# Beta held eight times per partition, so that the four transfers that add it move 4 KB rows

## The chip, the cores and the metric

The kernel runs on one core of a Trainium2 chip. The metric is the device time of one execution in microseconds (us), and a kernel's time is the median of its runs.

## What is computed

The input x has the shape (4, 1024, 128), in f32. Two layers follow one another. Each is added to its own input. Cut to what matters, in f32 throughout:

```python
# layer 1: attention without a softmax, 16 heads of 8
h = layernorm(x)
q, k, v = elu(h @ Wq + bq) + 1, elu(h @ Wk + bk) + 1, h @ Wv + bv
k = k / sqrt(sum(k * k, over a head) + 1e-6)
attn = q @ (k^T @ v)                    # per batch and head
y = h + attn @ Wo + bo
x = x + (y - mean(y)) / sqrt(var(y) + 1e-6) * gamma + beta

# layer 2: the 768 rows of each batch with the highest score go through a small product
h = layernorm(x)
scores = h @ w_router
top = top_k(scores, 768)
x = x + h.at[top].set(gelu(h[top] @ w_block))
```

The change touches the last line of layer 1 alone: how the sum x + beta comes to be.

## The kernel before

**Tiles.** A tile is 128 rows of one batch, one row per partition, 128 f32 values (512 B) in each. A batch has 8 tiles (`T`), and half a batch, 4 tiles (`TH`), is a unit `u`; there are 8 units (`U`). All work runs unit by unit. Every engine has its own list of steps, written out by hand at the end of its block, and semaphores tie them together, so no scheduler chooses an order.

**The steps on TensorE (PE).** Units are transposed (`transpose_h`), multiplied with the key and query weights (`k_proj`, `q_proj`), and once both halves of a batch have their normalised keys `attention_matrix(b)` (L1228) forms the product of keys and rows. `values`, `attention_out` and `y_half` (L1252, L1253) then give y.

**What the change touches.** The buffer `xb_sb` holds a second copy of x, loaded from DRAM in four transfers of one batch each (512 KB, L317, semaphores `xb_in[b]`) at the end of the list of loads of the SP queue. Four transfers issued from GpSimd (POOL) then add beta to it, one per batch (`add_beta(b)`, L394, semaphores `xb_set[b]`). Such a transfer reads `beta_sb` and `xb_sb`, adds, and writes `xb_sb`. `beta_sb` holds beta once in each partition (128 x 128, 64 KB in all, loaded at L312), and the source of the add names it eight times with a step of zero, so that a partition's row is made of eight runs of 512 B.

**What waits for them.** POOL waits for `beta_in` and `xb_in[0]` ahead of `add_beta(0)`, and its next steps are queued behind that wait: `scale_k(0)` and `scale_k(1)` (L400), which normalise the keys that `attention_matrix(0)` needs. The order on POOL is `add_beta(0)`, `scale_k(0)`, `scale_k(1)`, `add_beta(1)`, `add_beta(2)`, `scale_k(2)`, `scale_k(3)`, `add_beta(3)`, `scale_k(4)`, `roots2(0)` (L413), and so on. `scale_k(u)` itself waits for `key_norms(u // 2)` of VectorE (DVE, L799 and L801). The sums x + beta are read by POOL's `residual(0)` (L420, batch 0) and by DVE's `residual(u)` (L886), which wait for `xb_set[u // 2]`.

Of the kernel before, what the change touches and what calls it, by code (L numbers as in the profile page):

```python
# [12 lines left out]
P = 128  # L13
# [7 lines left out]
def preln_linear_attention_mod_ffn(nc, x, wq, bq, wk, bk, wv, bv, wo, bo, gamma, beta, w_router, w_block, out):  # L21
# [9 lines left out]
    B, L, D = x.shape  # L31
    assert D == P and HEADS * DEPTH == D and L % (2 * TH * P) == 0
    T = L // P
# [18 lines left out]
    with ExitStack() as ctx:  # L52
        def sb(name, shape, dt=F32):
            return ctx.enter_context(nc.sbuf_tensor(name, shape, dt))

        def sem(name):
            return ctx.enter_context(nc.semaphore(name))
# [3 lines left out]
        xb_sb = sb("xb_sb", [P, B * T, D])  # L61
# [46 lines left out]
        wz_sb = sb("wz_sb", [P, P + 1])  # L108
        wz_c = sb("wz_c", [P, P + 1])
        gamma_sb = sb("gamma_sb", [P, P])  # L110
        beta_sb = sb("beta_sb", [P, P])

        bias_rows = sb("bias_rows", [P, 3 * P])

# [14 lines left out]
        bias_in, bo_in, gamma_in, beta_in = sem("bias_in"), sem("bo_in"), sem("gamma_in"), sem("beta_in")  # L129
# [170 lines left out]
        @block.sync  # L300
        def _(sp):
            for u in range(U):
                b, a = u // 2, TH * (u % 2)
                if u == 0:
                    for h in range(2):
                        t = TH // 2 * h
                        sp.dma_start(x_sb[:, t:t + TH // 2, :], x_v[b, :, t:t + TH // 2, :]).then_inc(x0_in[h], 16)
                    sp.dma_start(w_sb[:, 2 * P:3 * P], wv).then_inc(w_in, 16)
                else:
                    sp.dma_start(x_sb[:, TH * u:TH * u + TH, :], x_v[b, :, a:a + TH, :]).then_inc(x_in[u], 16)  # L310
            sp.dma_start(wo_sb[:], wo).then_inc(wo_in, 16)
            sp.dma_start(beta_sb[:], beta.partition_broadcast(P)).then_inc(beta_in, 16)  # L312
            sp.dma_start(gamma_sb[:], gamma.partition_broadcast(P)).then_inc(gamma_in, 16)
            sp.dma_start(wz_sb[:, 0:P], w_block).then_inc(wz_in, 16)
            sp.dma_start(wz_sb[:, P:P + 1], w_router.unsqueeze(1)).then_inc(wz_in, 16)
            for b in range(B):
                sp.dma_start(xb_sb[:, T * b:T * b + T, :], x_v[b]).then_inc(xb_in[b], 16)  # L317
            for n, u in enumerate(MERGE_ORDER):
                sp.wait_ge(merged, n + 1)
                b, a = u // 2, TH * (u % 2)  # L320
                n = TH if u != LAST else TH // 2
                sp.dma_start(out_v[b, :, a:a + n, :], x_sb[:, TH * u:TH * u + n, :]).then_inc(out_stored, 16)
            sp.wait_ge(out_stored, 16 * (U + 1))

        @block.gpsimd
        def _(pool):
# [45 lines left out]
            def first_roots(h):  # L372
                _, m2 = stats(bn1, 2 * h, 2 * h + 2)
                t0, t1 = 2 * h, 2 * h + 2
                pool.wait_ge(first_stats_done, h + 1)
                link(nc.gpsimd.tensor_scalar(var1[:, t0:t1], m2, 1.0 / D, LN_EPS, ALU.mult, ALU.add))
                nc.gpsimd.tensor_tensor(r1[:, t0:t1], var1[:, t0:t1], minus_half[:].to_broadcast([P, 2]),
                                        ALU.pow).then_inc(first_r_done, 1)

            def roots1(g):  # L380
                us = ROOT_GROUPS[g]
                t0, t1 = TH * us[0], TH * us[-1] + TH
                _, m2 = stats(bn1, t0, t1)
                pool.wait_ge(x_stats, us[-1])
                link(nc.gpsimd.tensor_scalar(var1[:, t0:t1], m2, 1.0 / D, LN_EPS, ALU.mult, ALU.add))
                nc.gpsimd.tensor_tensor(r1[:, t0:t1], var1[:, t0:t1], minus_half[:].to_broadcast([P, t1 - t0]),
                                        ALU.pow).then_inc(r1_done, 1)

            def add_beta(b):

                if b == 0:
                    pool.wait_ge(beta_in, 16)
                pool.wait_ge(xb_in[b], 16)
                nc.gpsimd.dma_start(xb_sb[:, T * b:T * b + T], beta_sb[:].unsqueeze(1).to_broadcast([P, T, D]),  # L394
                                    accum_op=ALU.add).then_inc(xb_set[b], 16)

            def scale_k(u):
# [43 lines left out]
            roots1(4)  # L441
            masks()
            add_beta(0)
            scale_k(0)
            scale_k(1)
            add_beta(1)
            add_beta(2)
            scale_k(2)
            scale_k(3)
# [276 lines left out]
        def _(dve):  # L726
# [108 lines left out]
            def variances3(u):  # L835
                t0, t1 = TH * u, TH * u + TH
                _, m2 = stats(bn3, t0, t1)
                dve.wait_ge(x1_stats_done, u + 1)
                nc.vector.tensor_scalar(var3[:, t0:t1], m2, 1.0 / D, LN_EPS, ALU.mult, ALU.add).then_inc(var3_done, 1)  # L839
# [669 lines left out]
```

## Time and profile before

| | before |
|---|---|
| median of 3 runs | 91.2 us (91.19, 91.20, 91.83) |
| the profiled execution | 91.51 us |
| its span in the trace | 89.8 us |
| outside the span | 1.7 us |
| PE busy | 79.9 us (89%) |
| VectorE (DVE) busy | 80.9 us (90%) |
| ScalarE (ACT) busy | 66.9 us (75%) |
| GpSimd (POOL) busy | 52.8 us (59%) |
| granted TensorE clock, mean | 0.992 |

The profile is taken from one execution. Times in it are microseconds from the start of its span. PE stands for matmuls and PEld for weight loads. "SPq" marks the issuing of a DMA on the SP queue, and a row of a DMA says how long the issuing took. How long the transfer was under way is the time "to landing". The chain of work that ended last is followed back from the last instruction: what is not on it, or waits behind it, costs nothing.

### The profile page before, as it was taken

To read this page: it belongs to the slowest core of one execution; us is meant where nothing else is said; L and a number is where in the kernel's file an instruction comes from. 1 tells how busy PE (TensorE), PEld (TensorE's weight loads), DVE (VectorE), ACT (ScalarE), POOL (GpSimd) and SP (SyncE) were. 2 spreads that over 40 slices of the span, in tenths; PEclk is the share of its full clock that TensorE was granted. 3 is DMA by queue.
4 is the path that set the end of the run, shared out by engine and by line. 5 is a ranking of instruction groups with operands and counts; after the bars stand their busy time and mean duration, and the time that the engine had idled before them with its cause. 6 is when DMAs were issued, how large, how long until landed. Compare 5 with 4: busy or idle time off the path is not lost.

```text
span 89.8 us, 2397 instructions
## 1 busy us (share of the span) xinstructions
PE 79.9 (89%) x816; PEld 68.4 (76%) x816; DVE 80.9 (90%) x258; ACT 66.9 (75%) x186; POOL 52.8 (59%) x79
## 2 busy tenths in 40 slices
PE   4998689999999999999999599999999797999700
PEld 1335656976797997999999599999998797779600
DVE  4368999999797897999999999999999999999960
ACT  5003599998999996753539799999799696998700
POOL 5265885989992997659770979769838400000000
PEclk9999999999999999999999999999999999999996
DMA  0899969970999999900000000000000000348456
GB/s 24 233 256 319 280 168 319 290 189 7 143 127 140 139 143 136 112 10 0 0 0 0 0 7 0 0 4 7 0 4 0 0 7 10 107 121 236 138 149 180
DMA packets 18113, 8.99 MB, mean 100 GB/s; under 512 B 819, under 2 KB 18102, under 8 KB 18102
## 3 DMA queue, kind: packets, MB, share of 16 engines
q1 hardware_dynamic: 13232, 6.49, 26.7%
q0 software_dynamic: 4160, 2.10, 21.5%
q10 hardware_dynamic: 710, 0.26, 1.1%
q8 instruction: 6, 0.10, 0.4%
q14 instruction: 5, 0.04, 0.1%
HBM read 4.66 MB, written 2.10 MB: 75 GB/s over the span
## 4 chain that ended last, share of the span: by engine, by line
PE 46%; DVE 41%; issue 4%; ACT 3%; DVEq 1%; POOL 1%; ACTq 0%
DVE beats L918 11%; PE bank L1219 7%; PE bank L1211 7%; PE bank L1152 6%; DVE xb_sb L886 5%; DVE x_sb L941 5%; DVE bn L893 4%; PE bank L1252 4%; PE bank L1228 4%; PE bank L1253 4%; PE bank L1188 3%; PE bank L1271 3%; DVE beats L927 2%; DVE bn L818 2%; DVE x_sb L853 2%
## 5 line engine op out<-in xcount | busy, mean ns | idle before, releaser
L918 DVE TENSOR_SCALAR beats<-s_row,s_col 128x1024 bf16<-128x1024 f32 (+7 forms) x32 | 15.5, 541 | 0.0
L595 ACT ACTIVATE norm_sb<-xb_sb,shift,gain 128x128 f32<-128x128 f32 x32 | 13.2, 507 | 2.7 <-DVE shift L847 2.7
L1252 PE MATMUL bank<-M_sb,qT 128*128 128x128 f32 x64 | 12.5, 277 | 0.0
L1253 PE MATMUL bank<-back,hT 128*128 128x128 f32 x64 | 12.4, 275 | 0.0
L413 POOL TENSOR_TENSOR r<-var,minus_half 128x4 f32<-128x4 f32 x8 | 8.1, 1025 | 5.8 <-DVE var L833 5.5
L400 POOL TENSOR_TENSOR k_sb<-k_sb,k_rnorm 128x512 f32<-128x512 f32 x8 | 9.3, 1252 | 2.7 <-DVE k_rnorm L801 2.7
L426 POOL TENSOR_TENSOR r<-var,minus_half 128x4 f32<-128x4 f32 x8 | 9.1, 1194 | 2.9 <-DVE var L839 2.9
L1252 PEld LDWEIGHTS bank<-M_sb,qT 128*128 128x128 f32 x64 | 9.7, 192 | 0.2 <-ACT M_sb L558 0.2
L1253 PEld LDWEIGHTS bank<-back,hT 128*128 128x128 f32 x64 | 9.7, 192 | 0.0
L588 ACT ACTIVATE x_sb<-bank,r 128x128 f32<-128x128 f32 x32 | 9.2, 383 | 0.2 <-DVE s_col L901 0.2
L1219 PEld LDWEIGHTS bank<-w_c,hT 128*128 128x128 f32 x56 | 6.9, 192 | 2.1 <-ACT hT L513 1.1
L1271 PE MATMUL bank<-wz_c,hT 128*128 128x129 f32 x64 | 8.5, 278 | 0.0
L1219 PE MATMUL bank<-w_c,hT 128*128 128x128 f32 x56 | 7.3, 277 | 0.9 <-ACT hT L513 0.9
L1211 PE MATMUL bank<-hT,w_c 128*128 128x512 f32 x16 | 8.0, 593 | 0.0
L1228 PE MATMUL bank<-k_sb,norm_sb 128*128 128x128 f32 x64 | 7.8, 275 | 0.0
L1271 PEld LDWEIGHTS bank<-wz_c,hT 128*128 128x128 f32 x64 | 7.7, 192 | 0.0
L886 DVE SCALAR_TENSOR_TENSOR xb_sb<-bank,r,xb_sb 128x128 f32<-128x128 f32 x28 | 7.6, 338 | 0.0
L1228 PEld LDWEIGHTS bank<-k_sb,norm_sb 128*128 128x128 f32 x64 | 7.5, 192 | 0.0
L1292 PE MATMUL bank<-ident,beats 128*128 128x128 bf16 x108 | 6.8, 219 | 0.6 <-DVE dropped L936 0.6
L394 POOL DMA_DIRECT2D xb_sb<-beta_sb x4 | 7.0, 2060 | 0.1
L1152 PE MATMUL bank<-idle 128*128 128x512 bf16 x14 | 5.8, 601 | 1.3 <-DVE idle L735 1.3
L1292 PEld LDWEIGHTS bank<-ident,beats 128*128 128x128 bf16 x108 | 6.2, 98 | 0.9 <-DVE beats L918 0.8
(132 smaller groups left out, 216.7 us busy)
## 6 DMA issues: line engine op xcount, KB each, us to landing
xb_sb<-in_L_attn_x_dram SPq DMA_DIRECT2D x4, 512.0 KB, 6.8
xb_sb<-beta_sb POOLq DMA_DIRECT2D x4, 512.0 KB, 8.4
x_sb<-in_L_attn_x_dram SPq DMA_DIRECT2D x7, 256.0 KB, 5.2
out_dram<-x_sb SPq DMA_DIRECT2D x7, 256.0 KB, 2.3
x_sb<-in_L_attn_x_dram SPq DMA_DIRECT2D x2, 128.0 KB, 2.7
out_dram<-x_sb SPq DMA_DIRECT2D x1, 128.0 KB, 2.4
out_dram<-x_sb ACTq DMA_DIRECT2D x1, 128.0 KB, 2.5
w_sb<-in_L_attn_Wq_dram ACTq DMA_DIRECT2D x1, 64.0 KB, 2.5
```

The source lines that it names most:

```text
L400: nc.gpsimd.tensor_tensor(out_keys, keys, norms, ALU.mult).then_inc(keys_pool, 1)
L595: last = nc.scalar.activation(norm_sb[:, t], xb_sb[:, t], ACT.Identity, bias=shift3[:, t:t + 1], scale=gain3[:, t:t + 1])
L886: last = nc.vector.scalar_tensor_tensor(out=xb_sb[:, n], in0=bank_of(("y", u))[:, t * P:(t + 1) * P], scalar=r2[:, n:n + 1], in1=xb_sb[:, ...
L918: nc.vector.tensor_scalar(beats[:, b % 2, J, P * J:T * P], s_row[:, b, P * J:T * P], s_J, None, ALU.is_le).then_inc(beats_done, 1)
L1152: nc.tensor.matmul(bank[:, 7, :], idle16[:, 0:P], idle16[:], start=True, stop=True)
L1211: nc.tensor.matmul(take(("q", u)), w_c[:, 0:P], hT[:, u], start=True, stop=True).then_inc(q_full, 1)
L1219: last = nc.tensor.matmul(o[:, t * P:(t + 1) * P], hT[:, u, t * P:(t + 1) * P], w_c[:, P:2 * P], start=True, stop=True)
L1228: last = nc.tensor.matmul(o[:, 0:P], norm_sb[:, T * b + t], k_sb[:, 2 * b + t // TH, t % TH], start=(t == 0), stop=(t == T - 1))
L1252: nc.tensor.matmul(o, qT[:, u, t * P:(t + 1) * P], M_sb[:, b], start=True, stop=False)
L1253: last = nc.tensor.matmul(o, hT[:, u, t * P:(t + 1) * P], back[:], start=False, stop=True)
L1271: last = nc.tensor.matmul(o[:, j * (P + 1):(j + 1) * (P + 1)], hT[:, u, t * P:(t + 1) * P], wz_c[:], start=True, stop=True)
L1292: last = nc.tensor.matmul(o[:, n * P:(n + 1) * P], beats[:, b % 2, J, I * P:(I + 1) * P], ident16[:], start=(I == J), stop=(I == T - 1))
```

## The change

`beta_sb` grows from 128 x 128 to 128 x 8 x 128: beta lies eight times, one after the other, in each partition (4 KB per partition, 512 KB in all). Its load reads the same 512 B of DRAM eight times for each partition, and it is issued later: behind gamma and the two loads of `wz_sb`, right ahead of the four loads of `xb_sb`. In `add_beta` both sides are now named as flat rows of 1024 values, so that source and destination of a partition are one run of 4 KB each. Sum, semaphores, and the order of all other work stay.

```diff
-        beta_sb = sb("beta_sb", [P, P])
+        beta_sb = sb("beta_sb", [P, T, D])
...
             sp.dma_start(wo_sb[:], wo).then_inc(wo_in, 16)
-            sp.dma_start(beta_sb[:], beta.partition_broadcast(P)).then_inc(beta_in, 16)
             sp.dma_start(gamma_sb[:], gamma.partition_broadcast(P)).then_inc(gamma_in, 16)
             sp.dma_start(wz_sb[:, 0:P], w_block).then_inc(wz_in, 16)
             sp.dma_start(wz_sb[:, P:P + 1], w_router.unsqueeze(1)).then_inc(wz_in, 16)
+            sp.dma_start(beta_sb[:], beta.partition_broadcast(P).unsqueeze(1).to_broadcast([P, T, D])).then_inc(beta_in, 16)
             for b in range(B):
                 sp.dma_start(xb_sb[:, T * b:T * b + T, :], x_v[b]).then_inc(xb_in[b], 16)
...
-                nc.gpsimd.dma_start(xb_sb[:, T * b:T * b + T], beta_sb[:].unsqueeze(1).to_broadcast([P, T, D]),
+                nc.gpsimd.dma_start(xb_sb[:, T * b:T * b + T].rearrange("p t d -> p (t d)"), beta_sb[:].rearrange("p t d -> p (t d)"),
                                     accum_op=ALU.add).then_inc(xb_set[b], 16)
```

The SP queue, which issues the loads, from the load of `wo_sb` to the stores (a row: line, what, shape of the destination; "-" before, "+" after):

```order
 L311 DMA wo_sb<-in_L_attn_Wo_dram 128x128
-L312 DMA beta_sb<-in_L_attn_beta_dram 128x128
-L313 DMA gamma_sb<-in_L_attn_gamma_dram 128x128
-L314 DMA wz_sb<-in_L_ffn_w_block_dram 128x128
-L315 DMA wz_sb<-in_L_ffn_w_router_dram 128x1
+L312 DMA gamma_sb<-in_L_attn_gamma_dram 128x128
+L313 DMA wz_sb<-in_L_ffn_w_block_dram 128x128
+L314 DMA wz_sb<-in_L_ffn_w_router_dram 128x1
+L315 DMA beta_sb<-in_L_attn_beta_dram 128x8x128
 L317 DMA xb_sb<-in_L_attn_x_dram 128x8x128 x4
```

Beta's load went from the place behind `wo_sb` to the place ahead of `xb_sb`, and became eight times as large. The three loads that it was ahead of each stand one place earlier.

POOL, from the last of the masks to the second `scale_k` pair:

```order
 L368 AFFINE_SELECT head_mask<-head_mask 128x128
-L394 DMA xb_sb<-beta_sb 128x8x128
+L394 DMA xb_sb<-beta_sb 128x1024
 L400 TENSOR_TENSOR k_sb<-k_sb,k_rnorm 128x512 x2
-L394 DMA xb_sb<-beta_sb 128x8x128 x2
+L394 DMA xb_sb<-beta_sb 128x1024 x2
 L400 TENSOR_TENSOR k_sb<-k_sb,k_rnorm 128x512 x2
```

Nothing moved on POOL. The four adds keep their places and change their shape. PE, DVE and ACT have the same lists as before.

## Rows read from the trace of the kernel before

**Rows 1.** The page: the span, and the chain that ended last by engine.

```profile
span 89.8 us, 2397 instructions
...
PE 46%; DVE 41%; issue 4%; ACT 3%; DVEq 1%; POOL 1%; ACTq 0%
```

**Rows 2.** The chain that ended last, in order of time: start, us, what.

```profile
20.05 0.86 PE bank L1211 x2
...
34.85 0.24 PE bank L1234 x2
...
43.62 0.77 POOL r L413
```

**Rows 3.** Timeline of PE: start, us, engine, line, operation, out<-in.

```profile
23.36 1.04 PE L1188 MATMUL bank<-ident,norm_sb 128*128 128x128 f32 x8
24.23 1.95 PE L1228 MATMUL bank<-k_sb,norm_sb 128*128 128x128 f32 x16
```

**Rows 4.** Timeline of the SP queue's issuing.

```profile
9.62 0.43 SPq L315 DMA_DIRECT2D wz_sb<-in_L_ffn_w_router_dram  x1
10.09 5.39 SPq L317 DMA_DIRECT2D xb_sb<-in_L_attn_x_dram  x4
```

**Rows 5.** Timeline of POOL around the adds, idle time before and its releaser in brackets.

```profile
19.92 1.75 POOL L394 DMA_DIRECT2D xb_sb<-beta_sb  x1
21.11 2.71 POOL L400 TENSOR_TENSOR k_sb<-k_sb,k_rnorm 128x512 f32<-128x512 f32 x2
23.17 3.74 POOL L394 DMA_DIRECT2D xb_sb<-beta_sb  x2
28.53 2.11 POOL L400 TENSOR_TENSOR k_sb<-k_sb,k_rnorm 128x512 f32<-128x512 f32 x2 [1.62 <-DVE k_rnorm L801]
30.59 1.53 POOL L394 DMA_DIRECT2D xb_sb<-beta_sb  x1
31.93 1.31 POOL L400 TENSOR_TENSOR k_sb<-k_sb,k_rnorm 128x512 f32<-128x512 f32 x1
...
37.58 1.27 POOL L420 TENSOR_TENSOR xb_sb<-norm_sb,xb_sb 128x512 f32<-128x512 f32 x1
```

**Rows 6.** Timeline of DVE: the norms that `scale_k` waits for.

```profile
20.72 0.29 DVE L801 SCALAR_TENSOR_TENSOR k_rnorm<-k_tmp,k_seed 128x128 f32<-128x128 f32 x1
...
31.55 0.29 DVE L801 SCALAR_TENSOR_TENSOR k_rnorm<-k_tmp,k_seed 128x128 f32<-128x128 f32 x1
```

**Rows 7.** DMA issues: out<-in, queue, count, KB each, median us to landing.

```profile
beta_sb<-in_L_attn_beta_dram SPq DMA_DIRECT2D x1, 64.0 KB, 3.9
...
wz_sb<-in_L_ffn_w_block_dram SPq DMA_DIRECT2D x1, 64.0 KB, 3.0
```

**Rows 8.** Line L317, the first load of xb_sb alone: issue, and time to landing.

```profile
L317 SPq DMA_DIRECT2D xb_sb<-in_L_attn_x_dram x1: 434/434/434, 10.1 to 10.1; - x1
...
DMA to landing us min/median/max: 5.5/5.5/5.5
```

**Rows 9.** Line L317, the last load of xb_sb alone: issue, and time to landing.

```profile
L317 SPq DMA_DIRECT2D xb_sb<-in_L_attn_x_dram x1: 1619/1619/1619, 13.9 to 13.9; - x1
...
DMA to landing us min/median/max: 6.8/6.8/6.8
```

**Rows 10.** Line L394, the four adds together: time to landing.

```profile
DMA to landing us min/median/max: 6.9/8.4/11.3
```

**Rows 11.** Stretches: bounds, length, busy PE PEld DVE ACT POOL, clock, DMA share, GB/s.

```profile
12.00:12.50 0.50, 0.50 (x7) 0.50 (x6) 0.50 (x3) 0.50 (x2) 0.50 (x1) 1.00 0.52 125
...
15.50:16.00 0.50, 0.50 (x5) 0.50 (x6) 0.50 (x2) 0.50 (x2) 0.50 (x1) 1.00 1.20 291
```

**Rows 12.** DMA queues over the span: packets, MB, their time as share of 16 engines.

```profile
q1 hardware_dynamic: 13232, 6.49, 26.7%
q0 software_dynamic: 4160, 2.10, 21.5%
```

**Rows 13.** DMA queues in the stretch 22 to 39 us: the fetching of instructions.

```profile
q8 instruction: 2, 0.03, 0.7%
q14 instruction: 2, 0.02, 0.2%
```

**Rows 14.** Timeline of DVE: the steps that read x + beta of batches 1 to 3.

```profile
44.06 2.14 DVE L886 SCALAR_TENSOR_TENSOR xb_sb<-bank,r,xb_sb 128x128 f32<-128x128 f32 x8
...
50.63 2.15 DVE L886 SCALAR_TENSOR_TENSOR xb_sb<-bank,r,xb_sb 128x128 f32<-128x128 f32 x8
...
61.30 2.15 DVE L886 SCALAR_TENSOR_TENSOR xb_sb<-bank,r,xb_sb 128x128 f32<-128x128 f32 x8
```

## The prediction

> **What bounds the kernel now.** I read the page first. The span is 89.8 us, and the chain that ended last is PE for 46% and DVE for 41%; POOL holds 1% of it [rows 1]. The chain in order of time then tells what is critical where: from 20.05 to 34.85 us, over all the stretch in which the change acts on POOL's list, every piece is PE, one after the other with nothing between, and POOL's only piece that matters comes at 43.62, a root of 0.77 us [rows 2]. The timeline of PE shows the one step there that needs POOL's work: `attention_matrix(0)` starts at 24.23, and the transposes ahead of it start at 23.36 and are recorded for 1.04, so PE comes to it without a gap [rows 3]. The timeline of POOL shows when its part is done: `add_beta(0)` is issued at 19.92 and takes 1.75, and `scale_k(0)` and `scale_k(1)` run from 21.11 to 23.82 (21.11 + 2.71) [rows 5]. So the keys are there 0.41 us before PE wants them (24.23 - 23.82).
>
> **What the change adds.** Beta's load has 512 KB where it had 64, and all four loads of `xb_sb` are behind it. It takes the slot that the router weights' issue has now, 9.62, or the next one near 10.09 [rows 4]: one load is taken out ahead of it, so it is issued at about 9.6 and the first load of `xb_sb` again near 10.1. The question is how far the landing of `xb_sb` slips.
>
> Now the first load lands at 10.09 + 5.5 = 15.6 [rows 4, 8] and the last at 13.9 + 6.8 = 20.7 [rows 9]. Four loads, three steps between them: 5.1 / 3 = 1.7 us for each 512 KB. Beta's load has the same bytes and the same 512 B pieces, so I take 1.7 for it. From below it is 0: around 12 us the DMA engines are not full, with a share of 0.52 and 125 GB/s against 1.20 and 291 GB/s at 15.5 [rows 11], and a load issued sooner can fill that hole. From above it is 5.5, a whole load from issue to landing, as if nothing overlapped [rows 8]. The first batch of `xb_sb` then lands at 17.3 (15.6 to 21.1), the last at 22.4.
>
> POOL wants batch 0 at 19.92, where it issues `add_beta(0)` today, so at 17.3 there are 2.6 us to spare. Batches 1 and 2 land at about 19.0 and 20.7 and are wanted from 23.17 on; batch 3 lands at 22.4 and is wanted at 30.59 [rows 5]. Cost 0. What hides it is POOL's own list up to 19.92. The cover ends like this: queued behind `add_beta(0)` are the two `scale_k`, and behind those `attention_matrix(0)` on PE. From the issue of the add to `scale_k(0)` are at most 1.19 us today (21.11 - 19.92), the pair takes 2.71, and PE wants it at 24.23. So the add may start as late as 24.23 - 2.71 - 1.19 = 20.3 before PE waits. At the upper bound of 21.1 it would cost 0.8.
>
> Gamma and the two loads of `wz_sb` are issued 0.47 earlier each (9.62 against 10.09 is the step of that queue) and nobody waited for them. Cost and gain 0.
>
> **What the change removes.** Each add names 128 runs of 4 KB where it named 1024 of 512 B. The page has 4160 packets for 2.10 MB on the queue of GpSimd's transfers, about 512 B each [rows 12]. Two things can shrink.
>
> The first is POOL's time to build them: 1.75, 3.74 for two, 1.53, together 7.0 us [rows 5]. No row has an add of 128 runs. From below the gain is 0, from above it is all 7.0. But what counts is what waits behind, and there it is another engine each time. `scale_k(0)` starts at 21.11 because DVE's norms end at 20.72 + 0.29 = 21.01; `scale_k(4)` starts at 31.93 because DVE's end at 31.84 [rows 5, 6]; `scale_k(2)` sat idle for 1.62 until DVE's norms of batch 1 [rows 5]. What can come sooner is the end of a `scale_k` that runs while an add is being built: the pair at 21.11 is recorded with 2.71 us against 2.11 for the pair at 28.53, that is 0.6, and the one at 31.93 with 1.31 against about 1.06, that is 0.25 [rows 5]. The first makes the slack before `attention_matrix(0)` 1.0 where it was 0.4. PE has no gap there to close, so the gain is 0.
>
> The second is the transfers themselves. They are 21.5% of 16 engines over 89.8 us for 4160 packets: 0.215 x 16 x 89.8 / 4160 = 74 ns for 512 B, against 0.267 x 16 x 89.8 / 13232 = 29 ns on the load queue [rows 12]. With long runs they may come nearer to the latter. But no add lands later than 11.3 us after its issue [rows 10]: batch 0 by 31.2 at the latest and read from 37.58; batch 1 by 34.5, read from 44.06; batch 2 by about 36 (the second of the pair issued from 23.17, so at some 24 to 25), read from 50.63; batch 3 by 41.9, read from 61.30 [rows 5, 14]. Over 6 us are spare everywhere. Gain 0.
>
> **Sum.** 0 for the later load, 0 for the shorter issuing, 0 for the shorter transfers: the span stays at 89.8 and the profiled execution at 91.5 (91.51 before, 1.7 of it outside the span). That execution lay 0.3 over the median of the three runs, so for the median I say 91.2.
>
> **The rivals.**
>
> *A, the change doesn't do what it says:* the adds are still cut into pieces of 512 B. Nothing in the trace excludes it, since no row has a longer piece. Then 4160 packets stay, POOL's rows stay, and only the load slips. 91.2 as well. Chance 10%.
>
> *B, slower, beta's load is much slower than a plain one,* because 1024 pieces read the same 512 B. For it: beta's 64 KB took 3.9 us to land, the 64 KB of `w_block` issued 0.94 later took 3.0 [rows 7]. Were all of that 0.9 the price of reading one place, eight times as much is 7.2 us beyond the 1.7. `xb_sb` lands at 24.5, the limit is 20.3, and PE waits 4.2 us in a stretch in which it is the chain: 95.4. It decides from a landing of 20.3 on, that is when beta's load takes 4.7 us and not 1.7. Against it: the small loads were queued behind x, and in the half microsecond in which most of them moved the engines carried 125 / 0.52 = 240 GB/s per full share, as at 15.5 with 291 / 1.20 = 242 [rows 11]. Chance 4%.
>
> *C, slower, a 4 KB piece with an add takes longer per byte than eight of 512 B.* The batch that is nearest to its limit is batch 2: counted from the first issue, 36 - 19.92 = 16 us are used of 50.63 - 19.92 = 30.7 [rows 5, 14]. It decides from a factor of 1.9. At 2.2 DVE would wait about 16 x 2.2 - 30.7 = 4.5 us: 95.7. No row speaks for it, and the page's loads with 29 ns rather speak against. Chance 2%.
>
> *D, slower, the fetching of instructions waits behind long packets.* In the stretch of the adds 4 packets of instructions came through the same engines [rows 13]. Each could wait for one piece in progress, at 74 ns now and at most 8 x 74 = 590 ns then: 4 x 0.52 = 2.1 us if all of it hit a critical engine, 93.3. The Trainium skill (DMA: Bandwidth & Descriptors, "Queues, rings and completion order") says that an engine drains a whole packet of one queue before it turns to another, which is what this case would need. Against it, PE is without a gap on the chain from 20.05 to 34.85 [rows 2] though some of these fetches fall there, so they come well ahead of need. Chance 2%.
>
> *E, faster, POOL's relief reaches the chain.* The bound is what the `scale_k` steps give back, 0.6 + 0.25 = 0.85, and perhaps the root at 43.62 [rows 2, 5] comes sooner by as much again: down to 89.5. It would need a stretch in which PE or DVE really wait for POOL, and between 20 and 35 there is none; the root follows a DVE step. Chance 5%.
>
> **How the numbers follow.** The forecast of no change with merged runs has 77%, A with the same time 10%, B, C and D 8% on the slower side, E 5% on the faster one. About 1% is what a measurement of this kernel can tell from no change. Within 1% (90.3 to 92.1): 0.87. Slower: 0.08. Faster: 0.05. Where all terms are 0 the range is that of the medians: the runs before lie from 91.19 to 91.83, and the 0.8 of the upper bound of the load's slip, or the 0.6 of the first `scale_k` pair, would be the largest part of a neighbour. I say 90.7 to 91.8.
>
> **What would show it.** The queue of GpSimd's transfers has near 512 packets of 4 KB and not 4160 (else A). The adds' rows at L394 are well under 1.75 us. The last load of `xb_sb` lands at about 22.4. POOL still issues `add_beta(0)` at 19.9 with no wait for a DMA ahead of it (else B), and `attention_matrix(0)` still starts at 24.2. The adds land sooner than 6.9 to 11.3 us after issue (else C), and no step at L886 waits for a DMA. Wrong would be a POOL or PE row near 20 to 24 us that waits for the load, or a span that changes with PE's stretch up to 35 us unchanged, since I have no term for that.

## The result, and the profile after

The changed kernel is slower by a tenth, where no change was forecast.

| | before | after |
|---|---|---|
| median of 6 runs | 91.36 us (91.19 to 91.83) | 101.57 us (100.51 to 102.07) |
| ratio, 95% interval | | 1.109 (1.103 to 1.115) |
| span of the profiled execution | 89.8 us | 99.9 us |
| GpSimd (POOL) busy | 52.8 us | 50.1 us |
| granted TensorE clock, mean | 0.992 | 0.955 |

Some runs lie over 1.5% above the fastest of the same kernel: medians and ranges are of all runs, but ratios leave those out, and where only one other run is left no ratio is given.

The timeline of POOL of the changed kernel, which answers to [rows 5]:

```profile
19.45 0.45 POOL L368 TENSOR_SCALAR_AFFINE_SELECT head_mask<-head_mask 128x128 f32<-128x128 f32 x1
29.11 1.07 POOL L394 DMA_DIRECT2D xb_sb<-beta_sb  x1 [9.21 <-DMA xb_sb<-in_L_attn_x_dram]
29.91 2.41 POOL L400 TENSOR_TENSOR k_sb<-k_sb,k_rnorm 128x512 f32<-128x512 f32 x2
31.96 2.09 POOL L394 DMA_DIRECT2D xb_sb<-beta_sb  x2
```

POOL is ready for `add_beta(0)` at 19.90 and waits 9.2 us, until 29.11, for the first load of `xb_sb`. The two `scale_k` are queued behind it, and TensorE waits for them. Its timeline, against [rows 3]:

```profile
23.45 1.04 PE L1188 MATMUL bank<-ident,norm_sb 128*128 128x128 f32 x8
32.42 3.75 PE L1228 MATMUL bank<-k_sb,norm_sb 128*128 128x128 f32 x16 [7.94 <-POOL k_sb L400]
```

`attention_matrix(0)` starts at 32.42 where it started at 24.23, and takes 3.75 us where it took 1.95. The chain in order of time no longer runs through TensorE ahead of this step. It goes over the issuing on the SP queue and then has one piece of 18 us:

```profile
9.77 0.43 SPq L315
10.20 0.04 issue
10.24 18.26 DMA xb_sb<-in_L_attn_x_dram
28.50 0.02 issue
28.54 0.56 issue
29.11 1.07 POOL xb_sb L394
30.18 2.16 POOL k_sb L400 x2
32.34 0.09 issue
32.42 3.75 PE bank L1228 x16
36.18 0.99 PE bank L1219 x8
```

The step behind it stood here in the chain of the kernel before:

```profile
26.18 0.89 PE bank L1219 x8
```

So 10.0 us (36.18 - 26.18) of the 10.1 by which the span grew are lost by the end of `attention_matrix(0)`: 8.2 by its later start, 1.8 by its length.

The load itself is in the DMA issues (first row: the loads of `xb_sb`, 6.8 us before), and the rate at which it runs is in the stretches (columns as in [rows 11], the last two are DMA share and GB/s):

```profile
xb_sb<-in_L_attn_x_dram SPq DMA_DIRECT2D x4, 512.0 KB, 16.8
...
beta_sb<-in_L_attn_beta_dram SPq DMA_DIRECT2D x1, 512.0 KB, 17.1
```

```profile
12.00:13.00 1.00, 1.00 (x8) 0.66 (x6) 1.00 (x5) 1.00 (x4) 1.00 (x1) 1.00 0.24 44
...
17.00:18.00 1.00, 1.00 (x11) 1.00 (x10) 1.00 (x3) 0.97 (x3) 0.85 (x6) 1.00 0.26 44
...
26.00:27.00 1.00, 0.00 (x0) 0.00 (x0) 0.93 (x4) 0.39 (x2) 0.00 (x0) 1.00 0.92 277
```

Beta's load lands 17.1 us after its issue, at 26.9. While it is alone (12 to 23 us) the engines move 27 to 45 GB/s, microsecond by microsecond, and once the loads of `xb_sb` have their turn it is 277. From 13 to 23 us all pieces but two are of 512 B, 73 in a microsecond:

```profile
DMA packets 730, 0.37 MB, mean 37 GB/s; under 512 B 2, under 2 KB 730, under 8 KB 730
```

The first load of `xb_sb` lands at 28.5 (10.24 + 18.3), 12.9 us later than before.

The adds did become what the change says, see the queues and the times to landing, against [rows 12] and [rows 10]:

```profile
q0 software_dynamic: 576, 2.10, 10.8%
```

```profile
DMA to landing us min/median/max: 4.5/6.8/8.4
```

576 packets replace 4160. Their time is 0.108 x 16 x 99.9 / 576 = 300 ns each, for about 4 KB in most of them, half of the 8 x 74 = 592 ns for the same bytes before.

### The profile page after: what moved, and what is told of

It is laid out like the page before. It is cut to its first block, busy times and chain, and to the rows that moved or that the text cites. A ratio compares the mean times of both kernels' runs of the same rounds, so it can differ in the third digit from the quotient of the medians.

```text
span 99.9 us, 2397 instructions
## 1 busy us (share of the span) xinstructions
PE 81.7 (82%) x816; PEld 70.1 (70%) x816; DVE 80.6 (81%) x258; ACT 67.5 (68%) x186; POOL 50.1 (50%) x79
## 4 chain that ended last, share of the span: by engine, by line
DVE 45%; DMA 18%; PE 13%; SPq 9%; POOL 6%; issue 5%; DVEq 1%; POOLq 0%
DMA xb_sb<-in_L_attn_x_dram 18%; DVE beats L918 13%; DVE xb_sb L886 7%; PE bank L1228 6%; DVE bn L893 5%; SPq L310 5%; DVE x_sb L941 4%; DVE bn L818 3%; DVE beats L927 2%; POOL r L413 2%; POOL k_sb L400 2%; PE bank L1219 2%; DVE bank L860 2%; PE bank L1253 2%; PE bank L1252 2%
## 5 line engine op out<-in xcount | busy, mean ns | idle before, releaser
L1228 PE MATMUL bank<-k_sb,norm_sb 128*128 128x128 f32 x64 | 9.6, 314 | 7.9 <-POOL k_sb L400 7.9
L918 DVE TENSOR_SCALAR beats<-s_row,s_col 128x1024 bf16<-128x1024 f32 (+7 forms) x32 | 15.6, 543 | 0.0
L1228 PEld LDWEIGHTS bank<-k_sb,norm_sb 128*128 128x128 f32 x64 | 9.1, 227 | 8.1 <-POOL k_sb L400 8.1
L400 POOL TENSOR_TENSOR k_sb<-k_sb,k_rnorm 128x512 f32<-128x512 f32 x8 | 8.8, 1151 | 6.1 <-DVE k_rnorm L801 6.1
L813 DVE TENSOR_TENSOR vk_sb<-bank,head_mask 128x128 f32<-128x128 f32 x4 | 1.2, 288 | 10.9 <-PE bank L1234 10.9
L394 POOL DMA_DIRECT2D xb_sb<-beta_sb x4 | 4.0, 1151 | 9.2 <-DMA xb_sb<-in_L_attn_x_dram 9.2
L554 ACT COPY hk_sb<-bank 128x128 f32<-128x128 f32 x4 | 1.1, 279 | 9.8 <-PE bank L1228 9.8
## 6 DMA issues: line engine op xcount, KB each, us to landing
beta_sb<-in_L_attn_beta_dram SPq DMA_DIRECT2D x1, 512.0 KB, 17.1
```

The costliest lines, as they stand in the source:

```text
L400: nc.gpsimd.tensor_tensor(out_keys, keys, norms, ALU.mult).then_inc(keys_pool, 1)
L918: nc.vector.tensor_scalar(beats[:, b % 2, J, P * J:T * P], s_row[:, b, P * J:T * P], s_J, None, ALU.is_le).then_inc(beats_done, 1)
L1228: last = nc.tensor.matmul(o[:, 0:P], norm_sb[:, T * b + t], k_sb[:, 2 * b + t // TH, t % TH], start=(t == 0), stop=(t == T - 1))
```

## The experiments

In all of them the kernel before ran on the same chip; its median was 91.4 to 91.6 us.

### The load alone

```diff
-                nc.gpsimd.dma_start(xb_sb[:, ...].rearrange("p t d -> p (t d)"), beta_sb[:].rearrange("p t d -> p (t d)"),
+                nc.gpsimd.dma_start(xb_sb[:, T * b:T * b + T], beta_sb[:, 0].unsqueeze(1).to_broadcast([P, T, D]),
```

> Only one part of the change: beta is loaded eight times (512 KB, the same 512 B of DRAM over and over, at its new place), but the adds read the first copy with a step of zero, as before (128 x 8 x 128). Theory N (the load is slow because all 1024 pieces read one place in DRAM, and POOL's wait in add_beta(0) passes it on): as the changed kernel, 100.5 to 102, POOL idle some 9.2 us ahead of the first add, 4160 packets on GpSimd's queue. Theory F (the flat adds have a part in it): well below 101, by as much as the flat adds cost.

102.54 us (four runs, 100.89 to 103.27; no interval of the ratio), half a microsecond over the range that I had expected. The wait is there again, ahead of adds with the shape and the issuing time of before:

```profile
29.56 1.75 POOL L394 DMA_DIRECT2D xb_sb<-beta_sb  x1 [9.93 <-DMA xb_sb<-in_L_attn_x_dram]
```

So the loss does not need the flat adds. The runs lie too far apart to tell whether these change some tenths of a microsecond; the next run tells it.

### The same bytes from distinct rows

```diff
-            sp.dma_start(beta_sb[:], beta.partition_broadcast(P).unsqueeze(1).to_broadcast([P, T, D])).then_inc(beta_in, 16)
+            sp.dma_start(beta_sb[:], x_v[0]).then_inc(beta_in, 16)
```

> The changed kernel, but the 512 KB of beta_sb are filled from batch 0 of x, all of it distinct rows, and so wrong numbers are added: beta is left out. Same bytes, same 1024 pieces of 512 B, same place in the queue. Theory N: the load takes 1.7 us as those of xb_sb, the first load of xb_sb lands at about 17.3, and the time is that of the kernel before, 90.9 to 91.8. Theory L (any further 512 KB ahead of xb_sb costs this): about 101. Its adds are flat, so it also shows what flat adds are worth alone: 0 by my prediction.

91.40 us, ratio 0.999 (0.996 to 1.002). The loss is gone, with the load at the same place, of the same size and in the same pieces:

```profile
20.14 1.07 POOL L394 DMA_DIRECT2D xb_sb<-beta_sb  x1
21.41 2.11 POOL L400 TENSOR_TENSOR k_sb<-k_sb,k_rnorm 128x512 f32<-128x512 f32 x2 [0.20 <-DVE k_rnorm L801]
23.47 1.75 POOL L394 DMA_DIRECT2D xb_sb<-beta_sb  x2
```

```profile
beta_sb<-in_L_attn_x_dram SPq DMA_DIRECT2D x1, 512.0 KB, 5.1
```

The load lands in 5.1 us, and the first load of `xb_sb` at 9.77 + 6.4 = 16.2. The run also shows the flat adds with nothing in their way: issuing takes 1.07 and not 1.75, `scale_k(0)` and `scale_k(1)` take 2.11 and not 2.71, and POOL then sits idle 0.2 us for VectorE's norms. The time does not move.

### Two rows as the source

```diff
+            row = x[0, 0:1, :]
+            sp.dma_start(beta_sb[:].rearrange("p (k n) d -> p k n d", n=2),
+                         bass.AP(tensor=row.tensor, offset=row.offset, ap=[[0, P], [0, T // 2], [D, 2], [1, D]])).then_inc(beta_in, 16)
```

> As rows_8 with two rows (1 KB of DRAM), each read four times by every partition; beta is left out. Theory N with a limit per place: twice the rate of one row, the load takes 6 us and not 12, the first load of xb_sb lands at about 22.5 where it was 28.5, and the time is 91.4 + 2.2 (limit 20.3) = 93 to 95, without much of a fall of TensorE's clock. Theory Z: about 101.

92.86 us, ratio 1.016 (1.011 to 1.020), just under the 93 to 95 expected. The first microsecond of the load, the stretch from 12 to 17 us, and POOL behind it:

```profile
12.00:13.00 1.00, 1.00 (x9) 0.89 (x8) 1.00 (x5) 1.00 (x4) 1.00 (x1) 1.00 0.28 89
```

```profile
DMA packets 354, 0.35 MB, mean 70 GB/s; under 512 B 1, under 2 KB 354, under 8 KB 354
```

```profile
22.14 1.07 POOL L396 DMA_DIRECT2D xb_sb<-beta_sb  x1 [2.43 <-DMA xb_sb<-in_L_attn_x_dram]
```

It is 89 GB/s at first and 70 on average over these five microseconds, where one row gave 37, and POOL waits 2.4 us and not 9.2. The pieces in a microsecond are as many as with one row, 71 against 73, but of 1 KB each. So this run alone leaves open whether the limit is one on the place or one on the pieces.

### Eight rows, in one piece and apart

As above with `n=8`, once with a step of one row (`[D, 8]`, the source is 4 KB in one) and once with a step of three (`[3 * D, 8]`, eight separate pieces).

> The changed kernel, but every partition gets the first eight rows of x (4 KB of DRAM in one piece, read by all 128 partitions) in place of eight times beta: beta is left out. Theory N with a limit per place in DRAM: the eight places share the load, so it is up to eight times as fast and the time is near 91 to 92. Theory Z (it is the repeated reading by all partitions, a step of zero between partitions, however wide the source is): about 101.

> Every partition gets rows 0, 3, 6, ... 21 of x, eight separate pieces of 512 B; beta is left out. 1024 pieces as with beta, on eight places and not one. In the runs so far the pieces per us were about the same for one row (512 B each) and for two rows in one (1 KB each), some 75 to 80. Theory N1 (a limit for each place): eight places, up to eight times the rate, 91 to 92. Theory N2 (a limit on the pieces of a load that all partitions read from the same few places, whatever their number or size): 1024 pieces again take 12 to 13 us, 100 to 102.

91.35 us, ratio 1.000 (0.998 to 1.003), with the rows in one; 91.36 us, ratio 0.999 (0.995 to 1.003), with the rows apart. The load lands 5.5 and 5.6 us after its issue. In the run with the rows apart it still has 1024 pieces of 512 B, named by all partitions alike:

```profile
12.00:13.00 1.00, 1.00 (x5) 0.48 (x5) 1.00 (x5) 1.00 (x4) 1.00 (x1) 1.00 0.82 235
```

235 GB/s, more than five times the rate of one row. Pieces of the loads behind it may be in this figure, but not in the time to landing, 5.6 us against 17.1. That settles N1 (a limit for each place) against N2 (a limit on such pieces, on however many places): neither the number of pieces nor the step of zero between partitions is slow, but the number of places is what counts.

### One row of another tensor, and a row for each partition

```diff
+                         bass.AP(tensor=row.tensor, offset=row.offset, ap=[[0, P], [0, T], [D, 1], [1, D]])).then_inc(beta_in, 16)
```

> The changed kernel, but the one row read by all 1024 pieces is the first of x in place of beta, which is left out. Theory N: the place is slow because it is read over and over, whatever tensor it belongs to: as the changed kernel, 100.5 to 102.5. If it were something about beta's own small tensor: 91.4.

```diff
+            sp.dma_start(beta_sb[:], x[0, 0:P, :].unsqueeze(1).to_broadcast([P, T, D])).then_inc(beta_in, 16)
```

> Partition p gets row p of x eight times; beta is left out. 1024 pieces of 512 B on 128 places, each read eight times in a row by one engine. Theory N1: nothing is read by two engines at the same time and a place is asked for 4 KB in all, so the load is as fast as a plain one, 91 to 92. If the repeated reading of a place by the same engine is slow too (a step of zero inside the partition): between 93 and 101.

One row of x: 101.31 us, ratio 1.105 (1.095 to 1.114), so beta's tensor is nothing special. A row for each partition: 91.35 us, ratio 0.996 (0.993 to 0.999), so a step of zero within a partition is not slow either. The stretches of the one-row run have a surprise:

```profile
13.00:14.00 1.00, 1.00 (x6) 0.47 (x5) 1.00 (x5) 1.00 (x3) 0.86 (x1) 1.00 1.08 35
```

The rate is as low as with beta, 35 GB/s, but the DMA share is 1.08 and not 0.24. The share that packets take does not tell whether such a load is slow.

### Half the copies

```diff
-        beta_sb = sb("beta_sb", [P, T, D])
+        beta_sb = sb("beta_sb", [P, 4, D])
```

(the load and the adds follow: 256 KB, and two runs of 2 KB per partition)

> Beta four times per partition and not eight: a load of 256 KB out of the same 512 B, at the new place, and adds of two runs of 2 KB per partition. In the changed kernel the load ran at some 43 GB/s. If it is that rate per place that decides: 256 KB take 6 us, the first load of xb_sb lands near 22.4, POOL issues its first add near 22.9 and waits some 3 us, and the time is near that with two rows of DRAM as the source, 92.9. If the cost does not go with the bytes read from the one place, it stays near 101.

92.47 us, ratio 1.011 (1.006 to 1.016), near the 92.9 expected. The load lands at 9.35 + 9.9 = 19.25, 7.6 us ahead of the 26.9 of eight copies. 256 KB in 7.6 us is 34 GB/s. POOL issues the first add at 21.57, 7.5 us sooner, and the loss falls by 9.1 us. That is more than the wait alone, since `attention_matrix(0)` now waits 1.3 us and takes 2.02, with the clock still up (next experiment).

### The clock kept up

```diff
             def attention_matrix(b):
+                o = take(("M", b))
+                if b == 0:
+                    for _ in range(37):
+                        nc.tensor.matmul(o, idle16[:, 0:P], idle16[:], start=True, stop=True)
                 pe.wait_ge(*keys_set(2 * b))
                 pe.wait_ge(*keys_set(2 * b + 1))
-                o = take(("M", b))
```

> The changed kernel, and TensorE is given 37 idle bf16 matmuls (128x512) just ahead of attention_matrix(0), where it otherwise sits idle for 7.9 us and its granted clock falls to 0.50. They write the bank that the step itself takes. If the fall of the clock is a part of the loss of its own: attention_matrix(0) takes 1.8 and not 3.75 us, and the time is 2.0 less than the changed kernel, 99.3 to 99.8. If the clock only shows the wait: 101.5.

99.58 us, ratio 1.085 (1.078 to 1.092), 2.0 us less than the changed kernel. In the changed kernel the stretches of the wait show the granted clock (the third number from the right, ahead of DMA share and GB/s):

```profile
29.00:32.00 3.00, 0.00 (x0) 0.00 (x0) 0.00 (x0) 0.00 (x0) 2.89 (x4) 0.57 1.05 287
32.00:36.00 4.00, 3.58 (x17) 3.61 (x18) 0.00 (x0) 0.00 (x0) 2.05 (x3) 0.50 1.09 218
```

TensorE has done nothing since 24.5 us. The clock is still at 1.00 up to 29.0 and at 0.50, that is 1.2 GHz, from 29.5 on, and it stays there over `attention_matrix(0)`. With the idle matmuls:

```profile
25.22 7.93 PE L1227 MATMUL bank<-idle 128*128 128x512 bf16 x36
32.99 1.95 PE L1231 MATMUL bank<-k_sb,norm_sb 128*128 128x128 f32 x16
```

1.95 us again, so the fall of the clock is a fifth of the loss (2.0 of 10.2), on top of the wait that caused it. The trace of the changed kernel has nearly the same in it: 1.8 us in this step and 0.1 in the one behind (0.99 against 0.89). The Trainium skill (TensorE: Matmul & The Clock Gate, "Part 1: The HAM clock gate") says that an idle array is given 1.2 of its 2.4 GHz; the trace agrees with 0.50.

### The keys ahead of the add

```diff
-            add_beta(0)
             scale_k(0)
             scale_k(1)
+            add_beta(0)
```

> The changed kernel with one step moved on POOL: add_beta(0) stands behind scale_k(0) and scale_k(1) and not ahead of them. The load is as slow as before. If the loss goes by the order on POOL (keys behind an add that waits): attention_matrix(0) starts at 24.2 again, the wait for the load comes behind it, and the next to be late is attention_matrix(1), whose scale_k(2) and scale_k(3) stand behind add_beta(0) to add_beta(2): those are issued from 28.5 to about 32 and PE wants the keys at 31.1, so some 2 to 5 us are lost, 93.5 to 96.5, with a shorter fall of the clock. If the load harms in another way: near 101.

97.07 us, ratio 1.058 (1.050 to 1.065): 4.5 us of the loss come back, and the time is 0.6 us over the upper end that I had expected. TensorE's timeline:

```profile
23.69 1.95 PE L1228 MATMUL bank<-k_sb,norm_sb 128*128 128x128 f32 x16
...
35.22 3.55 PE L1228 MATMUL bank<-k_sb,norm_sb 128*128 128x128 f32 x16 [4.48 <-POOL k_sb L400]
```

`attention_matrix(0)` is on time, and the wait has moved to `attention_matrix(1)`, whose keys now stand behind three waiting adds. It waits 4.48 us and takes 3.55 where it took 1.95. These 6.1 us cover the 5.5 that are still lost. So here too the slow load does its harm through what is queued behind POOL's wait; a run with all keys ahead of the adds was not made.

### The position alone

```diff
-            sp.dma_start(beta_sb[:], beta.partition_broadcast(P)).then_inc(beta_in, 16)
             sp.dma_start(gamma_sb[:], gamma.partition_broadcast(P)).then_inc(gamma_in, 16)
             sp.dma_start(wz_sb[:, 0:P], w_block).then_inc(wz_in, 16)
             sp.dma_start(wz_sb[:, P:P + 1], w_router.unsqueeze(1)).then_inc(wz_in, 16)
+            sp.dma_start(beta_sb[:], beta.partition_broadcast(P)).then_inc(beta_in, 16)
```

> Position alone: beta once per partition (64 KB) and adds as before, but the load stands right ahead of the loads of xb_sb. At 43 GB/s its 64 KB take 1.5 us at either place. The first load of xb_sb lands within 1 us of 15.6 and POOL wants it at 19.9: no change, 90.9 to 91.8.

91.30 us, ratio 0.999 (0.995 to 1.003). Where the load stands is worth nothing at 64 KB.

### Copied on the chip

```diff
+            sp.dma_start(beta_one[:], beta.partition_broadcast(P)).then_inc(one_in, 16)
...
                 sp.dma_start(xb_sb[:, T * b:T * b + T, :], x_v[b]).then_inc(xb_in[b], 16)
+                if b == 0:
+                    sp.wait_ge(one_in, 16)
+                    sp.dma_start(beta_sb[:], beta_one[:].unsqueeze(1).to_broadcast([P, T, D])).then_inc(beta_in, 16)
```

> Beta is loaded once per partition (64 KB, at its old place), and a transfer within SBUF on the SP queue, behind the first load of xb_sb, spreads it to the eight copies; the adds are flat as in the changed kernel. If only the reading from one place in DRAM is slow: the loads of xb_sb are about where they were, POOL has no long wait, and the time is that of the kernel before, 90.9 to 91.8. If the spreading is as slow as the load of eight: about 101.

91.28 us, ratio 0.9964 (0.9933 to 0.9995).

```profile
beta_sb<-beta_one SPq DMA_DIRECT2D x1, 512.0 KB, 4.3
beta_one<-in_L_attn_beta_dram SPq DMA_DIRECT2D x1, 64.0 KB, 4.2
```

The same eight copies, made out of SBUF, land in 4.3 us and not in 17.1. The adds are flat, so this is the change with its intent kept and its price gone. Its median is 0.35% under that of the kernel before, and the interval ends 0.05% short of no change. I do not call that a gain: the run with a row for each partition shows the same ratio, and a difference of this size is no more than the kernel's runs vary among themselves.

### The source of the load, in one table

| source of `beta_sb` | places of 512 B | us to landing | time, us |
|---|---|---|---|
| beta, eight copies (the change) | 1 | 17.1 | 101.57 |
| one row of x, eight copies | 1 | 16.1 | 101.31 |
| beta, four copies (256 KB) | 1 | 9.9 | 92.47 |
| two rows of x | 2 | 10.1 | 92.86 |
| eight rows of x, in one piece | 8 | 5.5 | 91.35 |
| eight rows of x, apart | 8 | 5.6 | 91.36 |
| a row for each partition | 128 | 5.1 | 91.35 |
| distinct rows of x | 1024 | 5.1 | 91.40 |
| the copy of beta in SBUF | none in DRAM | 4.3 | 91.28 |

## Why the prediction was wrong, point by point

**What bounds the kernel, and where PE needs POOL.** Right. The step named, `attention_matrix(0)` at 24.23, is where the loss arose.

**The cost of beta's load: the step that failed.** It said "Beta's load has the same bytes and the same 512 B pieces, so I take 1.7 for it", from 0 to 5.5. Against the same load from distinct rows it landed 17.1 - 5.1 = 12.0 us later, so with that load's own 1.7 it took some 13.7 us, eight times the value and 2.5 times the upper bound (an estimate, since a load has no row for its time on the engines). Read directly, the first load of `xb_sb` landed 12.9 us later than before (28.5 against 15.6), where 1.7 was counted. What the loads of `xb_sb` and of beta had in common, bytes and pieces, doesn't set the rate. What they differed in does: one reads 1024 places and the other one place 1024 times. The upper bound was not a bound, because it came from a row of the other kind.

**The cover and its limit.** Right as a mechanism, and the limit was nearly right: the add may start as late as 20.3 us, said the prediction. In the changed kernel, with the shorter steps of the flat adds (0.80 us from the add to `scale_k(0)`, 2.41 for the pair) it is 24.23 - 2.41 - 0.80 = 21.0. The add came at 29.11, so 8.1 us late, and `attention_matrix(0)` started 8.2 us late. The slack of 2.6 us that I had counted was real (the run with distinct rows lost nothing; its first load of `xb_sb` landed at 16.2), but in the changed kernel that load landed 11.2 us behind the 17.3 on which it was counted.

**The clock.** Missing. The wait was long enough for the granted clock to fall, and 2.0 us of the 10.2 are that. Rival B had the wait in the right place but not this part.

**Rival B.** It was the right mechanism, with 4% for it and 95.4 us as its time, and its sign, POOL waiting for a DMA ahead of `add_beta(0)`, is what came. Its price took the difference of beta's and `w_block`'s landing, 0.9 us, times eight. The measured excess over distinct rows was 12.0 us for 512 KB from one place, 1.5 for each 64 KB and not 0.9. And what I put against it was misread. The trace of the kernel before held a hint in the half microsecond ahead of the one in [rows 11]:

```profile
11.50:12.00 0.50, 0.36 (x3) 0.36 (x4) 0.50 (x2) 0.50 (x3) 0.42 (x2) 1.00 0.21 41
```

41 GB/s at a share of 0.21 is what the changed kernel then showed for some 12 us (44 at 0.24 from 12 to 13). I took the hole around 12 us for a queue that had too little issued to it, and let the lower bound of 0 for beta's load rest on it. It may have been in part the loads of beta and gamma themselves, each 64 KB from one place. That is not shown, and 58 of the pieces in this half microsecond belong to neither load, being shorter than 512 B:

```profile
DMA packets 98, 0.02 MB, mean 41 GB/s; under 512 B 58, under 2 KB 98, under 8 KB 98
```

With distinct rows as the source beta is not loaded at all, and the hole is shallower but still there, 98 and 155 GB/s in the halves from 11.0 and 11.5 and 314 in the next, against 220, 41 and 125 before. No run left out gamma's load. The argument by GB/s per full share was no evidence at all: the run of the load alone moves 44 GB/s at a share of 0.20 from 13 to 14 us, 220 per full share at about a sixth of the rate of a plain load, and one row of beta and one row of x have the same low rate with a share of 0.24 and of 1.08.

**Shorter issuing, shorter transfers, position.** Right, each 0: the issuing fell from 7.0 to 4.0 us in all and the packets' time to half, and with distinct rows as the source the ratio is 0.999 (0.996 to 1.002). Moved alone, with its 64 KB, the load costs nothing.

**Rivals A, C, D and E.** A fell: 576 packets. C fell: a piece of 4 KB with an add takes half the time of eight of 512 B. D and E had nothing to show for them in the run with distinct rows.

## What to carry to other kernels

A load that repeats one short row of DRAM is not a load of its size: price it by how many distinct places it reads, and look in the trace for the GB/s of the stretch in which a broadcast load runs alone. Broadcast once and make further copies within SBUF. And before a load is put ahead of others in a queue, ask which engine's in-order list stops at its semaphore: here one wait on GpSimd held back keys that had nothing to do with beta, and TensorE's clock fell on top of it.

## What the runs showed of the hardware

- Filling all 128 partitions from one place of 512 B in DRAM ran at a mean of 37 GB/s with beta and 38 with a row of x (13 to 23 us); two places gave 89 GB/s in the first microsecond and a mean of 70 over the first five, and eight gave 235, near the 277 of a plain load. Between one and eight places the rate went with their number and not with pieces, partitions or steps of zero. Whether one place is as slow when few partitions read it, how far apart places have to be, and what in the memory sets the limit, was not tried.
- The same copy out of SBUF landed in 4.3 us for 512 KB: reading each partition's one row eight times there had no such price.
- With TensorE idle from 24.5 us on, its granted clock was 1.00 up to 29.0 and 0.50 from 29.5, and 16 matmuls then took 3.75 us and not 1.95.
- An accumulating transfer within SBUF took 300 ns for a piece of 4 KB and 74 ns for one of 512 B, and GpSimd's issuing of 512 KB fell from 1.75 to 1.07 us.
